# A convolutional attention block with a mixture of experts on one core: the last pair of batches taken batch by batch

## The chip, the core and the metric

One NeuronCore of a Trainium2 chip. The metric is the device time of one launch in microseconds, the median of several runs. Five engines work side by side, each on its own queue of instructions in order: TensorE (PE, matmuls into PSUM), VectorE (DVE), ScalarE (ACT), GpSimd (POOL, which reads and writes SBUF only) and SyncE (SP, which issues transfers). They meet by semaphores: an instruction adds to one when it is done, and a queue waits until one has reached a number.

## The reference, cut to what matters

Eight batches of 64 channels by 1024 tokens. First a channel attention, then a routed feed-forward part. In short, with the layer norms written out:

```python
x = x + conv_attention(layernorm_over_channels(x))      # per batch, 8 heads
t = to_tokens(x)                                        # (8, 1024, 64)
u = layernorm(t)
weights = softmax(mean(u, tokens) @ Wr + br)            # one routing row per batch
# scaled by capacity, softmax again, top 2 of 8 experts, softmax over the two
y = sum over the 2 experts of w_k * (gelu(u @ W1[k] + b1[k]) @ W2[k] + b2[k])
t = t + layernorm(y + u) * gamma + beta
```

The routing is by batch, so each batch uses two experts for all its tokens. In the last layer norm each token needs its mean of squares over the 64 channels (the mean itself is taken out by centred weights), and one reciprocal root of it.

## The kernel before, in words

Batches go in pairs, NP = 4 pairs p of batches b = 0, 1. In the feed-forward part a tile has 128 partitions: 64 channels of the first 512 tokens and 64 of the last 512; the 1024 columns are 512 of batch 0 and 512 of batch 1. A "step" is one expert k of one pair, step = 2p + k, eight in all. `up(step, b)` (L1155) multiplies by W1 into `h_ps[b]`, `gelu` (L387) brings it to `H` on ScalarE, `down(step, b)` (L1183) multiplies by W2 and adds into `y_ps`, on top of `residual3(p)` (L1169), which puts the residual there. The semaphore mm2 rises once a step, after the down of b = 1. GpSimd gathers the chosen experts' weights in advance (L470, L483).

When both experts of a pair are in `y_ps`, the last layer norm follows as a relay over engines:

- VectorE writes (y + c2) * gamma to `ZS` (`evac_z`, L828; L834), ScalarE squares y + c2 (`square_z`, L396; L406), the halves in opposite order.
- TensorE sums the squares over the channels (`rows3`, L1198; L996), ScalarE copies the rows (`evac_rows3`, L409; L413), TensorE turns them to columns with tokens on partitions (`columns3`, L1207; L1002).
- VectorE makes the variance (L840) and its reciprocal root by seven small instructions on 16 columns (`rsqrt`, L554: L557 to L567). GpSimd, and VectorE for the last pair, splits it in three bf16 parts (`split3`, L217: L220 to L223), TensorE turns these back (`turn3`, L1211; L1006), VectorE copies them (L853), and TensorE spreads them over the channels (`spread3`, L1048; L1011).
- VectorE scales `ZS` by the spread root (`scale_z`, L855; L858), and `add_residual` (L225; L230) adds T, which holds t + beta: GpSimd for pairs 0 to 2, VectorE for pair 3. Each addition releases the transfers of its batch (L263 on SyncE's queue; for the second half of the last pair's rows L436 on ScalarE's).

The order of TensorE's work is written by hand (L1232 to L1258): the relay of one pair is put between ups and downs of the next. After the last down there is no such work, and `keep_awake_at_end` (L1194) issues 7 and then 9 matmuls whose result nobody reads. The first layer norm of the feed-forward part is spread in another way: `spread2` (L1015; L1030) multiplies a root column, repeated 64 times as the weights, with the identity in float32.

## Time and profile before

| | us |
|---|---|
| median of 3 runs | 108.69 (108.67 to 108.73) |
| the profiled execution | 108.59 |
| its span (first to last instruction) | 106.8 |
| PE busy | 88.7 (83%) |
| DVE busy | 70.9 (66%) |
| ACT busy | 48.2 (45%) |
| POOL busy | 32.2 (30%) |

A busy share is an average over the span; what a late stage costs is read from its own rows. Times in the rows are from the span's start. In a timeline, rows of one kind that follow each other are merged with their count (x4), and the releaser in brackets is who ended the idle time before. PE rows overlap a little, since matmuls are pipelined; a float32 matmul has two records. The chain of waits gives each stretch of time to one instruction only.

### The profile page before, as it was taken

The numbers are of one execution on the slowest core, as the hardware profiler recorded it, in microseconds if no ns is written. First come the engines' busy times: TensorE is split into PE (matmuls) and PEld (weight loads), VectorE is DVE, ScalarE is ACT, GpSimd is POOL, SyncE is SP. The second block draws the span as 40 slices with busy tenths as digits, with TensorE's granted clock in tenths as the row PEclk, the third lists the DMA queues.
The fourth block names the chain that finished last, engine by engine and source line by source line (L and its number), as shares of the span: only waits on it lengthen the run. The fifth ranks groups of instructions, "written<-read, shape, count | busy, mean of one in ns | idle before, by whom it ended". The sixth has DMA issues, their size and how long they took to land.

```text
span 106.8 us, 2258 instructions
## 1 busy us (share of the span) xinstructions
PE 88.7 (83%) x748; PEld 47.8 (45%) x749; DVE 70.9 (66%) x258; ACT 48.2 (45%) x83; POOL 32.2 (30%) x77
## 2 busy tenths in 40 slices
PE   5967898998999999777976999599999999986200
PEld 1424776997665437355922237133333333242100
DVE  0098999842789978989999943714537256668920
ACT  0000946647321111103747899996795895510000
POOL 5000000005200000004428199956261900861400
PEclk9999999999999999999999999999999999999975
DMA  3899999400000000001420125680000080056065
GB/s 56 302 396 312 269 303 345 84 0 0 0 6 0 0 0 0 3 6 47 101 52 6 32 69 130 153 201 7 6 0 0 0 185 18 0 132 147 15 147 147
DMA packets 6554, 9.82 MB, mean 92 GB/s; under 512 B 1040, under 2 KB 3344, under 8 KB 6544
## 3 DMA queue, kind: packets, MB, share of 16 engines
q1 hardware_dynamic: 4848, 6.77, 24.1%
q10 hardware_dynamic: 1696, 2.92, 9.6%
q8 instruction: 6, 0.10, 0.4%
q14 instruction: 4, 0.03, 0.1%
HBM read 5.49 MB, written 2.10 MB: 71 GB/s over the span
## 4 chain that ended last, share of the span: by engine, by line
PE 58%; DVE 15%; ACTq 9%; ACT 7%; issue 5%; DVEq 1%
PE pC L1188 14%; PE pC L955 5%; ACTq L281 5%; PE pA L906 4%; PE pB L896 3%; PE pA L967 3%; PE pA L1163 3%; ACTq L276 3%; PE pB L1163 3%; PE pM L996 2%; DVE bst L644 2%; ACT SQ L406 2%; PE pC L1180 2%; PE pS L1030 2%; ACT U L290 2%
## 5 line engine op out<-in xcount | busy, mean ns | idle before, releaser
L457 POOL TENSOR_TENSOR LO<-UF,HI 128x512 f16<-128x512 f32 x8 | 9.2, 1157 | 23.5 <-ACT HI L324 22.6
L1188 PE MATMUL pC<-H,w2g 128*64 128x512 f32 x64 | 15.8, 602 | 0.0
L576 DVE BATCH_NORM_STATS2 bst<-XT 128x6 f32<-128x128 f32 x32 | 7.1, 282 | 5.2 <-DMA XT<-x_tok_dram 5.2
L230 POOL TENSOR_TENSOR XT<-XT,T 128x512 f32<-128x512 f32 x6 | 7.5, 1269 | 4.0 <-DVE XT L858 4.0
L1076 PE MATMUL pM<-wz 128*128 128x512 bf16 x25 | 7.1, 444 | 1.3 <-POOL wz L450 1.3
L393 ACT ACTIVATE H<-pA,b1s 128x1024 f32<-128x1024 f32 x6 | 6.7, 1111 | 2.5 <-PE pA L1163 2.3
L473 POOL COPY w1g<-w1hl 128x256 f16 x14 | 5.1, 403 | 8.1 <-issue 6.0
L324 ACT CAST HI<-UF 128x512 f16<-128x512 f32 x8 | 4.8, 619 | 6.0 <-DVE UF L677 6.0
L463 POOL TENSOR_TENSOR w1hl<-SQ,w1hl 128x512 f16<-128x512 f32 x2 | 2.3, 1154 | 17.2 <-DVE A L623 17.2
L644 DVE BATCH_NORM_STATS2 bst<-pA 128x6 f32<-128x128 f32 x32 | 6.9, 284 | 0.6 <-PE pA L967 0.5
L834 DVE TENSOR_SCALAR U<-pC,c,wsm 128x512 f32<-128x512 f32 x8 | 6.2, 801 | 1.4 <-PE pC L1188 0.9
L406 ACT ACTIVATE SQ<-pC,c 128x512 f32<-128x512 f32 x8 | 5.4, 685 | 3.8 <-PE pC L1188 3.0
L858 DVE TENSOR_TENSOR XT<-U,pS 128x512 f32<-128x512 f32 x6 | 4.1, 684 | 4.3 <-PE pS L1011 4.3
L638 DVE SCALAR_TENSOR_TENSOR T<-pC,cbs,X 128x512 f32<-128x512 f32 x8 | 5.7, 747 | 1.8 <-PE pC L955 1.8
L393 ACT ACTIVATE H<-pB,b1s 128x1024 f32<-128x1024 f32 x6 | 6.7, 1122 | 0.0
L1188 PEld LDWEIGHTS pC<-H,w2g 128*64 128x64 f32 x64 | 4.1, 136 | 5.9 <-issue 4.3
L331 ACT ACT_TABLE_LOAD x1 | 1.3, 1283 | 10.9 <-issue 10.9
L955 PE MATMUL pC<-U,MTs 64*64 64x512 f32 x32 | 6.1, 613 | 0.0
L290 ACT COPY U<-pA 128x1024 f32<-128x1024 f32 x4 | 4.0, 1012 | 3.4 <-PE pA L906 3.4
L319 ACT COPY SR<-pM 128x256 f32<-128x256 f32 x4 | 1.5, 372 | 9.0 <-PE pM L980 9.0
L967 PE MATMUL pA<-cst,T 128*128 128x128 f32 x32 | 5.0, 284 | 0.2 <-DVE bst L644 0.2
L594 DVE TENSOR_TENSOR UT<-XT,rt 128x512 f32<-128x512 f32 x8 | 5.1, 688 | 0.1
(219 smaller groups left out, 186.7 us busy)
## 6 DMA issues: line engine op xcount, KB each, us to landing
out_dram<-XT SPq DMA_DIRECT2D x14, 128.0 KB, 2.4
XT<-x_tok_dram SPq DMA_DIRECT2D x2, 512.0 KB, 9.3
X<-x_cha_dram SPq DMA_DIRECT2D x8, 128.0 KB, 11.0
X<-x_cha_dram ACTq DMA_DIRECT2D x8, 128.0 KB, 10.9
ST<-HI SPq DMA_DIRECT2D x6, 128.0 KB, 2.4
ST<-LO SPq DMA_DIRECT2D x6, 128.0 KB, 2.4
XT<-x_tok_dram SPq DMA_DIRECT2D x2, 256.0 KB, 4.8
XT<-x_tok_dram ACTq DMA_DIRECT2D x2, 256.0 KB, 5.1
```

Of the source, the lines that this page charges most:

```text
L230: engine.tensor_tensor(OUT[:, p, cols], V[:, p, cols], T[:, p, cols], ALU.add).then_inc(s_fin[2 * p + h], 1)
L393: nc.scalar.activation(H[:, step % 2, b, :], h_ps[b][:, :], ACT.Gelu, bias=bias, scale=1.0 / (S_U * S_W)).then_inc(s["gelu"], 1)
L406: nc.scalar.activation(SQ[:, p % 2, cols], y_ps[:, cols], ACT.Square, bias=c2[:, 2 * p + b:2 * p + b + 1]).then_inc(s["sq3"], 1)
L457: nc.gpsimd.tensor_tensor(LO[:, p, cols], UF[:, p, cols], HI[:, p, cols], ALU.subtract).then_inc(s["lo"], 1)
L576: return nc.vector.bn_stats(bst[:, p, j, :], XT[:, p, j * P:(j + 1) * P].rearrange("p (b c) -> p c b", b=2))
L644: last = nc.vector.bn_stats(bst2[:, p, j, :], tt[:, j * P:(j + 1) * P].rearrange("p (h c) -> p c h", h=2))
L834: nc.vector.tensor_scalar(ZS[:, p, cols], y_ps[:, cols], c2[:, i:i + 1], w("gamma"), ALU.add, ALU.mult).then_inc(s["zs"], 1)
L955: last = mm(half(cv[:, b * HALF:(b + 1) * HALF], h), half(MTs[:, p, :], b), half(U[:, p, h * HALF:(h + 1) * HALF], b), start=True, stop=True)
L967: last = nc.tensor.transpose(tt[:, j * P:(j + 1) * P], T[:, p, j * P:(j + 1) * P], cf("ident"))
L1076: mm(pM[:, :], wz[:, 0:P], wz[:, :], start=True, stop=True)
L1163: last = mm(h_ps[b][:, h * HALF:(h + 1) * HALF], w1g[h * C:(h + 1) * C, p % 2, k, b, a, :], src[h * C:(h + 1) * C, p, b * HALF:(b + 1) * H ...
L1188: last = mm(half(y_ps[:, b * HALF:(b + 1) * HALF], h), w2g[:, p % 2, b, k, :], H[:, step % 2, b, h * HALF:(h + 1) * HALF], start=False, st ...
```

## The change

Pair 3 is taken by batches. `unit(step, i)` gives for steps 6 and 7 the batch by the step and the expert by i: step 6 is both experts of batch 6 (the pair's first), step 7 both of batch 7. So batch 6 is whole in `y_ps` after step 6's downs. The relay of pair 3 is then run once per batch, in pieces of 128 columns (`rows_last`, `columns_last`, `variance_last`), its moments in `ps_last`. The reciprocal root is one GpSimd instruction per batch, a power with exponent -0.5 (`root_last`), and TensorE spreads it in the way of `spread2` (`spread_last`), without the split, the turn and the copy. `keep_awake_at_end` is gone. In step 7 `columns3` comes before down(6,0); after the last up the order of TensorE is written out. ScalarE takes over the evacuation of batch 7's `ZS` (`evac_z_last`), which needs gamma * c2 as its bias: one new VectorE instruction makes it (gc2) before the first `evac_z`. The additions: both of pair 2 go from GpSimd to VectorE, the first of pair 3 (batch 6) goes from VectorE to GpSimd.

```diff
@@ -143,6 +143,8 @@
         gtab = sb("gtab", [P, 1])
+        mhalf = sb("mhalf", [P, 1])
+        gc2 = sb("gc2", [P, 1])
@@ -163,6 +165,11 @@
             return ap.rearrange("p (q h b) -> p h q b", h=2, b=2)
+        def unit(step, i):
+            p, n = step // TOP, step % TOP
+            return (p, n, i) if p < NP - 1 else (p, i, n)
@@ -192,8 +199,9 @@
-        ps_rt3 = [q[0:3 * G2, 0:P // 2].bitcast(BF16) for q in (pS, pS, pS, pB)]
-        rb3 = [[pS[:, :], pS[:, :]]] * (NP - 1) + [[pB[:, HALF:N], pA[:, HALF:N]]]
+        ps_rt3 = [pS[0:3 * G2, 0:P // 2].bitcast(BF16)] * (NP - 1)
+        rb3 = [[pS[:, :], pS[:, :]]] * (NP - 2) + [[pS[:, :], pB[:, HALF:N]], [pA[:, 0:HALF], pA[:, HALF:N]]]
+        ps_last = [pM[:, 0:P], pB[:, 0:P]]
         ps_lg = [pM, pA[:, 0:HALF]]
@@ -207,7 +215,7 @@
         names = ("ones wz iota onesm brzz brz wrz wrd w1f wcp wcv bvz bvd gram gs tb u p1 p1s s_ps sms exs a_sb b1 b1s mt mts "
-                 "cbs conv t st sr w1p w1h w1l w2p w2v pow1 tt bt sc red2 pow2 rb hi lo lgm lg lr rexp1 rexp2 "
+                 "cbs conv t mh gc st sr w1p w1h w1l w2p w2v pow1 tt bt sc red2 pow2 rb hi lo lgm lg lr rexp1 rexp2 "
                  "half_tanh rx1 rx2 rx3 wkd top w1g "
@@ -378,19 +386,34 @@
+            def square_last(b):
+                act.wait_ge(s["mm2"], TOP * NP - 1 + b)
+                cols = slice(b * HALF, (b + 1) * HALF)
+                nc.scalar.activation(SQ[:, 1, cols], y_ps[:, cols], ACT.Square,
+                                     bias=c2[:, B - 2 + b:B - 1 + b]).then_inc(s["sq3"], 1)
+            def evac_rows_last(b):
+                act.wait_ge(s["row3"], NP + b)
+                act.wait_ge(s["mom3"], NP - 2)
+                nc.scalar.copy(RW[:, 1, b * P:(b + 1) * P], ps_last[b]).then_inc(s["rw3"], 1)
+            def evac_z_last():
+                act.wait_ge(s["gc"], 1)
+                nc.scalar.activation(ZS[:, NP - 1, HALF:N], y_ps[:, HALF:N], ACT.Identity, bias=gc2[:, :],
+                                     scale=w("gamma")).then_inc(s["zs"], 1)
             def gelu_bias(p, k, b):
                     return w("b1T")[:, bass.ds(first_expert(k, b), 1)]
-                act.wait_ge(s["b1d"], k + 1)
+                act.wait_ge(s["b1d"], TOP)
                 return b1s[:, k, 2 * p + b:2 * p + b + 1]
-            def gelu(p, k, b):
-                step = TOP * p + k
-                bias = gelu_bias(p, k, b)
-                act.wait_ge(s["mm1"], 2 * step + b + 1)
+            def gelu(step, i):
+                bias = gelu_bias(*unit(step, i))
+                act.wait_ge(s["mm1"], 2 * step + i + 1)
                 if step >= 2:
                     act.wait_ge(s["mm2"], step - 1)
-                nc.scalar.activation(H[:, step % 2, b, :], h_ps[b][:, :], ACT.Gelu, bias=bias,
+                nc.scalar.activation(H[:, step % 2, i, :], h_ps[i][:, :], ACT.Gelu, bias=bias,
                                      scale=1.0 / (S_U * S_W)).then_inc(s["gelu"], 1)
@@ -416,12 +439,12 @@
                     square_z(p - 1)
-                gelu(p, k, 0)
+                gelu(step, 0)
                 if k == 1 and p >= 1:
                     half_tanh()
-                gelu(p, k, 1)
+                gelu(step, 1)
                 if step == 0:
@@ -429,8 +452,10 @@
                     add_beta(p)
-            square_z(NP - 1)
-            evac_rows3(NP - 1)
+            for b in range(2):
+                square_last(b)
+                evac_rows_last(b)
+            evac_z_last()
             for b in range(2):
@@ -490,7 +515,16 @@
+            def root_last(b):
+                pool.wait_ge(s["mh"], 1)
+                pool.wait_ge(s["red3"], NP + b)
+                cols = slice(b * G2 // 2, (b + 1) * G2 // 2)
+                nc.gpsimd.tensor_tensor(r3[:, NP - 1, cols], v3[:, NP - 1, cols],
+                                        mhalf[:, 0:1].broadcast_to([P, G2 // 2]), ALU.pow).then_inc(s["pow3"], 1)
             nc.gpsimd.memset(wrbd[:, :], 0.0).then_inc(s["wrz"], 1)
+            nc.gpsimd.memset(mhalf[:, :], -0.5).then_inc(s["mh"], 1)
             nc.gpsimd.memset(brz[:, :], 0.0).then_inc(s["brzz"], 1)
@@ -535,8 +569,9 @@
                     add_residual(nc.gpsimd, pool, p - 1, 1)
-            add_residual(nc.gpsimd, pool, NP - 2, 0)
-            add_residual(nc.gpsimd, pool, NP - 2, 1)
+            root_last(0)
+            root_last(1)
+            add_residual(nc.gpsimd, pool, NP - 1, 0)
@@ -824,6 +859,7 @@
             dve.wait_ge(s["c2d"], 1)
+            nc.vector.tensor_tensor(gc2[:, :], c2[:, B - 1:B], w("gamma"), ALU.mult).then_inc(s["gc"], 1)
@@ -857,25 +893,34 @@
-            for p in range(NP):
-                if p < NP - 1:
-                    evac_z(p)
+            def evac_z_first():
+                dve.wait_ge(s["sq3"], 2 * NP - 1)
+                nc.vector.tensor_scalar(ZS[:, NP - 1, 0:HALF], y_ps[:, 0:HALF], c2[:, B - 2:B - 1], w("gamma"),
+                                        ALU.add, ALU.mult).then_inc(s["zs"], 1)
+            def variance_last(b):
+                dve.wait_ge(s["mom3"], NP + b)
+                nc.vector.tensor_scalar(v3[:, NP - 1, b * G2 // 2:(b + 1) * G2 // 2].rearrange("p (q r) -> p q r", r=2),
+                                        ps_last[b].rearrange("p (q r) -> p q r", r=32)[:, :, 0:2], 1.0, EPS_T,
+                                        ALU.mult, ALU.add).then_inc(s["red3"], 1)
+            for p in range(NP - 1):
+                evac_z(p)
                 if p >= 1:
                     scale_z(p - 1, 0)
-                if 1 <= p < NP - 1:
                     scale_z(p - 1, 1)
                 rstd3(p)
-                if p == NP - 2:
-                    evac_z(NP - 1)
-                if p == NP - 1:
-                    dve.wait_ge(s["pow3"], NP)
-                    dve.wait_ge(s["rt3"], NP - 2)
-                    split3(nc.vector, link, p % 2, 1, r3[:, p:p + 1, :], s["s3"])
                 rows3(p)
+            evac_z_first()
+            variance_last(0)
+            scale_z(NP - 2, 0)
             scale_z(NP - 2, 1)
+            variance_last(1)
+            add_residual(nc.vector, dve, NP - 2, 0)
+            add_residual(nc.vector, dve, NP - 2, 1)
             scale_z(NP - 1, 0)
+            dve.wait_ge(s["zs"], 2 * NP)
             scale_z(NP - 1, 1)
-            add_residual(nc.vector, dve, NP - 1, 0)
             add_residual(nc.vector, dve, NP - 1, 1)
@@ -1047,8 +1092,8 @@
                 pe.wait_ge(s["rr3"], p + 1)
-                if 2 * p + h >= 1 and p < NP - 1:
-                    pe.wait_ge(s["vv"], 2 * p + h)
+                if 2 * p + h >= 1:
+                    pe.wait_ge(s["vv"], min(2 * p + h, 2 * NP - 4))
                 spread(rb3[p][h], h * CH // 2, CH // 2, p).then_inc(s["rb3"], 1)
@@ -1152,15 +1197,15 @@
-            def up(step, b):
-                p, k = step // TOP, step % TOP
-                pe.wait_ge(s["w1g"], 2 * step + b - 1)
-                pe.wait_ge(s["gelu"], 2 * (step - 1) + b + 1)
+            def up(step, i):
+                p, k, b = unit(step, i)
+                pe.wait_ge(s["w1g"], 2 * (TOP * p + k) + b - 1)
+                pe.wait_ge(s["gelu"], 2 * (step - 1) + i + 1)
                 for n, (a, src, done) in enumerate(((0, HI, s["hi"]), (1, HI, s["hi"]), (0, LO, s["lo"]))):
                     for h in range(2):
-                        last = mm(h_ps[b][:, h * HALF:(h + 1) * HALF],
+                        last = mm(h_ps[i][:, h * HALF:(h + 1) * HALF],
                                   w1g[h * C:(h + 1) * C, p % 2, k, b, a, :],
@@ -1180,20 +1225,16 @@
-            def down(step, b):
-                p, k = step // TOP, step % TOP
-                pe.wait_ge(s["gelu"], 2 * step + b + 1)
-                pe.wait_ge(s["g2"], 2 * step + b + 1)
+            def down(step, i):
+                p, k, b = unit(step, i)
+                pe.wait_ge(s["gelu"], 2 * step + i + 1)
+                pe.wait_ge(s["g2"], 2 * (TOP * p + k) + b + 1)
                 for h in range(2):
                     last = mm(half(y_ps[:, b * HALF:(b + 1) * HALF], h), w2g[:, p % 2, b, k, :],
-                              H[:, step % 2, b, h * HALF:(h + 1) * HALF],
+                              H[:, step % 2, i, h * HALF:(h + 1) * HALF],
                               start=False, stop=(k == TOP - 1))
-                if b == 1:
+                if i == 1:
                     last.then_inc(s["mm2"], 1)
-            def keep_awake_at_end(n):
-                for _ in range(n):
-                    mm(h_ps[0][:, 0:HALF], cb("identb"), cb("sel")[:, 0:HALF], start=True, stop=True)
@@ -1210,9 +1251,32 @@
                 pe.wait_ge(s["s3"], p + 1)
-                if 1 <= p < NP - 1:
+                if p >= 1:
                     pe.wait_ge(s["vv"], 2 * p)
                 turn(ps_rt3[p], p % 2).then_inc(s["rt3"], 1)
+            def rows_last(b):
+                pe.wait_ge(s["sq3"], 2 * NP - 1 + b)
+                if b == 0:
+                    pe.wait_ge(s["red3"], NP - 1)
+                for q in range(4):
+                    last = mm(ps_last[b][32 * q:32 * (q + 1), :], cf("mean2"),
+                              SQ[:, 1, b * HALF + q * P:b * HALF + (q + 1) * P], start=True, stop=True)
+                last.then_inc(s["row3"], 1)
+            def columns_last(b):
+                pe.wait_ge(s["rw3"], NP + b)
+                nc.tensor.transpose(ps_last[b], RW[:, 1, b * P:(b + 1) * P], cf("ident")).then_inc(s["mom3"], 1)
+            def spread_last(b):
+                pe.wait_ge(s["pow3"], NP + b)
+                for k in range(CH // 2):
+                    for h in range(2):
+                        i = b * G2 // 2 + 2 * k + h
+                        last = mm(half(rb3[NP - 1][b][:, k * P:(k + 1) * P], h),
+                                  r3[:, NP - 1, i:i + 1].broadcast_to([P, C]), cf("ident"), start=True, stop=True)
+                last.then_inc(s["rb3"], 1)
@@ -1229,33 +1293,36 @@
-            for step in range(3, TOP * NP + 4):
+            for step in range(3, TOP * NP):
                 q, odd = (step - 5) // TOP, step % TOP
-                if step < TOP * NP:
-                    for b in range(2):
-                        up(step, b)
-                if step > TOP * NP and odd and q + 1 < NP:
-                    rows3(q + 1)
+                for i in range(2):
+                    up(step, i)
                 if odd and q >= 0:
                     spread3(q, 0)
-                if step < TOP * NP and odd and q + 1 >= 0:
+                if odd:
                     rows3(q + 1)
-                if step <= TOP * NP:
-                    if step % TOP == 1:
-                        residual3(step // TOP)
-                    down(step - 1, 0)
-                if step > TOP * NP and odd and q + 1 < NP:
+                    residual3(step // TOP)
+                if step == TOP * NP - 1:
                     columns3(q + 1)
+                down(step - 1, 0)
                 if odd and q >= 0:
                     spread3(q, 1)
-                if step < TOP * NP and odd and q + 1 >= 0:
+                if odd and step < TOP * NP - 1:
                     columns3(q + 1)
-                if step <= TOP * NP:
-                    down(step - 1, 1)
-                if not odd and 0 <= (step - 4) // TOP < NP:
-                    if step >= TOP * NP:
-                        keep_awake_at_end(7 if step == TOP * NP else 9)
+                down(step - 1, 1)
+                if not odd and step >= 4:
                     turn3((step - 4) // TOP)
+            down(TOP * NP - 1, 0)
+            turn3(NP - 2)
+            rows_last(0)
+            down(TOP * NP - 1, 1)
+            columns_last(0)
+            spread3(NP - 2, 0)
+            spread3(NP - 2, 1)
+            rows_last(1)
+            columns_last(1)
+            spread_last(0)
+            spread_last(1)
```

## Rows read from the trace of the kernel before

**Rows 1.** The page: the chain that ended last, by engine

```profile
PE 58%; DVE 15%; ACTq 9%; ACT 7%; issue 5%; DVEq 1%
```

**Rows 2.** The chain in order of time: start us, us, what

```profile
65.59 0.90 PE pM L1030 x16
...
88.43 0.33 PE pS L1011 x4
...
89.13 2.73 PE pC L1188 x12
...
92.01 1.46 PE pA L1196 x6
...
95.39 1.26 DVE nwt L557
```

**Rows 3.** Timeline, 87 to 93 us: start, us, engine line op [idle before <-releaser]

```profile
87.23 0.37 ACT L413 COPY RW<-pM 128x256 f32<-128x256 f32 x1
...
88.80 0.69 DVE L858 TENSOR_TENSOR XT<-U,pS 128x512 f32<-128x512 f32 x1 [1.81 <-PE pS L1011]
...
89.40 0.17 DVE L840 TENSOR_SCALAR v<-pM 128x16 f32<-128x16 f32 x1
...
91.10 0.20 POOL L220 CAST R<-r 128x16 bf16<-128x16 f32 x1 [5.41 <-DVE r L567]
...
92.03 2.50 POOL L230 TENSOR_TENSOR XT<-XT,T 128x512 f32<-128x512 f32 x2
```

**Rows 4.** Timeline, the last scalings and additions

```profile
99.66 0.67 DVE L858 TENSOR_TENSOR XT<-U,pB 128x512 f32<-128x512 f32 x1
99.82 1.27 POOL L230 TENSOR_TENSOR XT<-XT,T 128x512 f32<-128x512 f32 x1 [3.22 <-DVE XT L858]
100.26 0.67 DVE L858 TENSOR_TENSOR XT<-U,pA 128x512 f32<-128x512 f32 x1
100.86 1.38 DVE L230 TENSOR_TENSOR XT<-XT,T 128x512 f32<-128x512 f32 x2
```

**Rows 5.** Timeline, pair 0's evacuation, squares and moments

```profile
67.12 0.81 DVE L834 TENSOR_SCALAR U<-pC,c,wsm 128x512 f32<-128x512 f32 x1
...
67.76 1.26 ACT L406 ACTIVATE SQ<-pC,c 128x512 f32<-128x512 f32 x2
...
69.07 0.64 PE L996 MATMUL pM<-SQ,cst 128*32 128x256 f32 x8 [1.21 <-ACT SQ L406]
```

**Rows 6.** Timeline of POOL alone, at 67 us and at 78 us

```profile
67.06 1.16 POOL L457 TENSOR_TENSOR LO<-UF,HI 128x512 f16<-128x512 f32 x1
...
78.07 1.04 POOL L489 TENSOR_TENSOR w2g<-w2c,wk 128x64 f32<-128x64 f32 x4
```

**Rows 7.** Timeline, 48.6 to 51 us

```profile
48.66 1.16 POOL L457 TENSOR_TENSOR LO<-UF,HI 128x512 f16<-128x512 f32 x1 [21.20 <-ACT HI L324]
...
49.01 0.89 DVE L746 TENSOR_TENSOR rout<-rout,rsm 128x64 f32<-128x64 f32 x1
...
50.90 0.22 DVE L752 TENSOR_TENSOR rout<-rout,rsm 128x64 f32<-128x64 f32 x1
```

**Rows 8.** Groups by form on POOL: busy us, mean ns | idle before

```profile
L221 POOL TENSOR_TENSOR rd<-r,R 128x16 f32<-128x16 f32 x3 | 0.7, 218 | 0.2
```

**Rows 9.** SyncE's last two transfers: duration ns, first and last start; landing

```profile
L263 SPq DMA_DIRECT2D out_dram<-XT x2: 852/933/1014, 102.3 to 103.2; - x2
...
DMA to landing us min/median/max: 3.2/3.2/3.3
```

**Rows 10.** ScalarE's two transfers: the same columns

```profile
L436 ACTq DMA_DIRECT2D out_dram<-XT x2: 522/542/562, 101.7 to 102.3; - x2
...
DMA to landing us min/median/max: 2.4/3.1/3.8
```

**Rows 11.** Busy us by stretch: PE PEld DVE ACT POOL, PEclk, DMA share, GB/s

```profile
68.00:70.00 2.00, 0.93 (x12) 0.41 (x14) 0.81 (x1) 2.00 (x4) 1.33 (x2) 1.00 0.74 175
...
100.00:104.00 4.00, 0.00 (x0) 0.00 (x0) 2.24 (x4) 0.00 (x0) 1.09 (x1) 0.88 0.40 91
```

## The prediction

> **What bounds the kernel now.** I read three views in this order: the chain of waits, to see who sets the end; the timeline of the last 20 us, to see each step of the tail; then the rows of transfers and of two earlier stretches. The page's chain gives TensorE over half of the span [rows 1], but the last 15 us are another thing. Down to 91.86 us the chain is TensorE, matmul after matmul: three half downs of 0.91 us each end it [rows 2]. From there to the last addition, which ends at 102.24, it is a relay: keep-awake matmuls, moments, the root on VectorE, its split and turn, spread, scaling, addition. The whole root and turn of pair 3 stands between 95.39 and the first scaling by it at 99.66, 4.27 us [rows 2, 4]. In it one instruction on 16 columns takes 1.26 us [rows 2]; it stood beside a GpSimd addition of pair 2 and got through when that ended. The last transfer is issued at 103.2, 0.9 us after the last addition, because SyncE was still issuing pair 2's, whose second half GpSimd added only from 99.82 to 101.09 [rows 4, 9]. It lands 3.2 us later, 0.4 us before the span's end.
>
> The profiled execution took 108.59 us against a median of 108.69; its span is 106.8, so 1.79 us lie around it. All times below are on the span's clock of before; the sum ends at 108.59 and I forecast with the same 1.79.
>
> **Before the last pair.** Steps up to 6 keep their order and sizes on all engines (two experts of one batch cost what one expert of two batches does: same shapes, and the last gathers, pair 3's, are done at 79.1 [rows 6], two us before their first use). The memset of the -0.5 column lies where GpSimd waits for the first loads: nothing. One edit here is not free. gc2 is a new VectorE instruction between the last normalising multiply and pair 0's evacuation, which starts at 67.12 [rows 5]. By size it would cost 0.05 to 0.2 us. But both its inputs are in SBUF, and GpSimd is in a subtraction that reads SBUF from 67.06 to 68.22 [rows 6]. What that does is seen at 49.01: a VectorE tensor_tensor of 64 columns with both inputs in SBUF took 0.89 us, ending 0.08 after the GpSimd subtraction that had begun before it; the same form with GpSimd idle took 0.22 [rows 7]. So gc2 ends at about 68.25 and the evacuation starts about 1.1 us late. ScalarE's square of that half, which waits for it, starts at 69.05 instead of 68.34 (0.4 us of the delay was waiting for ScalarE anyway: its two squares run 67.76 to 69.02), and TensorE's moments, which had idled 1.21 us for that square [rows 5], start 0.7 us late. From there the chain is TensorE and the same evacuations, with no slack before 86 us. I take **+0.7 us**; the other end is 0.05.
>
> The Trainium skill, page "SBUF — State Buffer", section "Who interferes with whom", states this as a rule: a VectorE instruction with two SBUF inputs contends with a GpSimd instruction that reads SBUF, and the later one blocks for the whole of the other. The trace's 0.89 against 0.22 us agrees. Without the rule gc2 would be priced at 0.05, and the forecast would be 0.65 us lower.
>
> **The tail, step by step** (without the 0.7). Step 7 issues the turned moments of pair 2 before down(6,0) rather than after. They wait for the row copy that ends at 87.60 [rows 3], take 0.37 (the gap between the rows at 88.76 and 89.13 [rows 2]) and let down(6,0) start at 88.0; it ends near 88.95, and the spread of pair 1's second half (0.33) at 89.28 instead of 88.76. VectorE's multiply of that half waits for it, and the root of pair 2 stands behind that multiply, so its moments being early buys nothing: multiply at 89.3, moments at 89.9, and the split on GpSimd, done by 92.05 before (the addition behind it starts at 92.03 [rows 3]), at 92.6. TensorE meanwhile does down(6,1) and down(7,0), to 91.1, and now has turn3(2) next. It **waits 1.5 us** there, with down(7,1) queued behind it. Then turn 0.25, rows_last(0) 0.4 (half the columns of the 0.64 us row [rows 5]; bounds 0.3 to 0.64), down(7,1) to 94.15, columns_last(0) to 94.4, both spreads of pair 2 to 95.05. Before, the last down ended at 91.86; this costs 2.3 us, and the rest has to earn it back.
>
> Batch 7: square 0.69 to 94.9, rows_last(1) 95.05 to 95.45, copy of 128 columns 0.26 (bound 0.37 [rows 3]) and transposes to 96.1, variance on VectorE to 96.3. VectorE has by then scaled both halves of pair 2 (94.75 to 96.0; 512-column instructions follow each other every 0.60 us, 99.66 to 100.26 [rows 4]). The square, rows and copy of batch 6 lie under down(7,1).
>
> GpSimd splits pair 2 to 92.6, adds pair 1's residual for 2.50 [rows 3] to 95.05, and only then takes root_last(0), though its variance is there at 94.6. The **price X of a power** on 8 columns is in no row. The nearest rows: a plain GpSimd subtraction of 16 columns takes 0.22 [rows 8], and the whole root of a pair on VectorE takes 1.70 (89.40 to the cast at 91.10 [rows 3]). I take 0.6: eight values a partition are few, so the fixed part of 0.2 weighs most, with some 50 ns for each value; both ends stay for the range. root_last(1) is ready at 96.35, but VectorE has just started the first addition of pair 2 (two SBUF inputs), to 96.9. Either one goes first; in both orders the two follow each other: power to 96.9 + X, second addition to 97.5 + X, scaling of batch 6 to 98.1 + X. TensorE's spread_last(1) needs 0.9 (16 matmul records in the same form [rows 2]) and ends at 97.9 + X, in time for scaling of batch 7. GpSimd's addition of batch 6 runs from 98.15 + X for 1.27 [rows 4]; VectorE's own addition of batch 7, ready at 98.7 + X, again has two SBUF inputs and ends 0.6 after it, at **100.0 + X**. If VectorE isn't held there, GpSimd's is last, at 99.4 + X.
>
> With X = 0.6 and the 0.7 of gc2 the last addition ends at 101.3, against 102.24. What goes: the stalled instruction of 1.26 us and, behind it, the ten small instructions, turn, copy and spread up to the scaling (96.65 to 99.66, 3.0 us [rows 2, 4]); what comes: the 1.5 us wait of TensorE, two additions on VectorE ahead of the last scalings, gc2.
>
> **After the last addition.** Before it is 4.56 us to the span's end. Pair 2's four transfers now start at 97.7 and 98.8, and are issued when the last pair's come, so SyncE no longer runs 0.9 us late. ScalarE's second transfer is the other end: it was issued at 102.3, in time, and took 3.8 [rows 10]. Bounds 3.6 to 4.4; I take 3.9, since four transfers share the end and not six. Span 101.3 + 3.9 = 105.2, time **107.0 us**, 1.6 us or 1.5% faster.
>
> **Rivals.**
> (1) gc2 isn't held, since it has a single column or gets its read in first: 106.35. For it: no row is so small. Against: rows 7, and that GpSimd's subtraction begins 0.06 us before it. Chance 0.25; with X near 0.22 and no hold at the last addition, this reaches 105.4.
> (2) The power is dear, and the kernel slower. Above X = 1.2 the two powers follow each other without a gap other than an addition, and the end is 98.8 + 2X; before is met at 102.2, X = 1.7. Both powers stand in line on GpSimd behind 2.5 us of additions, and VectorE's additions with two SBUF inputs are held beside them, so nothing hides them. At X = 2.5 the time is 103.8 + 0.7 + 3.9 + 1.8 = 110.2. For it: a power is a function and not one pass of an adder; no row shows it. Against: only 8 values a partition. Chance 0.17.
> (3) TensorE falls to 1.2 GHz in the thinner tail, as the fillers are gone: from 92.6 on turn, rows, down, columns and spreads double, 2.9 us on the path, 109.9. Against it: the granted clock is full in 68 to 70 us at 0.93 of 2 us busy, and falls only well after the last matmul of before (0.88 over 100 to 104) [rows 11]. Chance 0.08.
> (4) The batches don't do what they should: batch 6's early start is eaten by the wait at turn3(2). That is in the sum already. If the sum is short of another 1.6 us of such waits the result is no change: chance 0.05.
> The forecast, X between 0.2 and 1.7 with gc2 held, has 0.45.
>
> **How the numbers follow.** A measurement of this kernel tells some 0.2% (0.2 us) from no change. Faster: 0.45 + 0.25 and the part of (2) just below the break-even and of (3), 0.03: 0.73. Same 0.07. Slower: most of (2) and (3), 0.20. The range goes from 105.5 (rival 1 with small X) to 109.2 (X = 2.0), which leaves out most of (3) and the upper half of (2), and a little below.
>
> **What the profile after would show.** gc2's row at about 1.1 us, and moments of pair 0 at 69.8; if it is 0.2 and they stand at 69.1, rival 1. TensorE idle some 1.5 us before pair 2's turn. Two powers on GpSimd: their duration is X itself, the first right behind pair 1's additions. VectorE's last addition recorded at 1.2 to 1.3 us beside GpSimd's. The last transfer issued within 0.2 us of the last addition. A granted clock below 1 between 90 and 98 would be rival 3. The prediction is wrong if the power costs over 1.7 us, or if the chain before 86 us moves by anything but gc2.

## The result

Over 4 runs the changed kernel took 107.06 us (median), the kernel before 108.71 on the same chip; the ratio is 0.9843 (in brackets here and below, its 95% interval: [0.9825, 0.986]), 1.6% faster. The forecast was 107.0. That the number came out is in good part luck: a power cost 1.65 us and more where the forecast had 0.6, and what follows the powers was shorter than forecast by nearly as much as that adds.

The profiled execution of the changed kernel took 109.52 us, with a mean granted clock of 0.954 and TensorE at 1.2 GHz in two stretches; the others on that chip had 0.992 to 0.995 and spans of 105.2 to 105.3. So the tail is read from other executions, and this one for what happens at 67 to 76 us. Its page, the chain by engine and the clock in 40 slices (compare [rows 1]: GpSimd is new in the chain):

```profile
PE 55%; DVE 14%; ACTq 9%; ACT 8%; POOL 6%; issue 5%; POOLq 0%; DVEq 0%
...
PEclk9999999999999999999999999957999999999755
```

Its timeline at pair 0's evacuation, which answers [rows 5] and [rows 6]. L862 is the new multiply, gc2; L429 the squares, L1041 the moments:

```profile
67.20 1.11 DVE L862 TENSOR_TENSOR gc<-c,wsm 128x1 f32<-128x1 f32 x1
...
69.06 0.69 ACT L429 ACTIVATE SQ<-pC,c 128x512 f32<-128x512 f32 x1 [0.54 <-DVE U L870]
...
69.80 0.64 PE L1041 MATMUL pM<-SQ,cst 128*32 128x256 f32 x8 [1.86 <-ACT SQ L429]
```

One column takes 1.11 us, the moments start at 69.80 instead of 69.07, and TensorE's wait for them grew from 1.21 to 1.86 us. Busy us by stretch of the same execution (the columns of [rows 11]):

```profile
68.00:70.00 2.00, 0.20 (x4) 0.16 (x8) 1.75 (x3) 1.46 (x3) 1.40 (x2) 1.00 0.71 167
70.00:72.00 2.00, 2.00 (x14) 0.62 (x8) 0.00 (x0) 2.00 (x4) 1.26 (x4) 0.62 0.86 200
72.00:74.00 2.00, 2.00 (x8) 0.59 (x6) 0.22 (x2) 1.07 (x2) 1.17 (x5) 0.53 0.11 26
74.00:76.00 2.00, 2.00 (x16) 0.50 (x12) 1.18 (x7) 0.34 (x1) 0.47 (x3) 1.00 0.00 0
```

The column behind POOL's is the granted clock. TensorE is busy for 0.20 of 2 us (before 0.93 [rows 11]), and then works for some three microseconds at half clock. That is some 1.6 us of the execution's extra 2.4 (its tail starts that much later than in the next run's trace); the rest is the last spread, 1.82 us instead of 1.09. The thin stretch alone does not settle it: in the next run TensorE is busy for 0.18 of the same 2 us, and the clock stays at 1.00.

### The profile page after: what moved, and what is told of

The parts are those of the page before. It is cut to its first block, busy times and chain, and to the rows that moved or that the text cites. A ratio compares the mean times of both kernels' runs of the same rounds, so it can differ in the third digit from the quotient of the medians.

```text
span 107.7 us, 2282 instructions
## 1 busy us (share of the span) xinstructions
PE 89.9 (84%) x764; PEld 48.8 (45%) x764; DVE 68.6 (64%) x248; ACT 49.2 (46%) x85; POOL 34.4 (32%) x79
## 4 chain that ended last, share of the span: by engine, by line
PE 55%; DVE 14%; ACTq 9%; ACT 8%; POOL 6%; issue 5%; POOLq 0%; DVEq 0%
PE pC L1233 12%; PE pC L1000 5%; ACTq L289 5%; PE pA L951 4%; PE pB L941 3%; PE pA L1012 3%; POOL r L523 3%; PE pA L1208 3%; ACTq L284 3%; PE pB L1208 3%; DVE bst L679 2%; POOL XT L238 2%; DVE U L870 2%; PE pS L1075 2%; PE pC L1225 2%
## 5 line engine op out<-in xcount | busy, mean ns | idle before, releaser
L1233 PE MATMUL pC<-H,w2g 128*64 128x512 f32 x64 | 17.0, 637 | 0.0
L1121 PE MATMUL pM<-wz 128*128 128x512 bf16 x25 | 7.8, 482 | 1.3 <-POOL wz L475 1.3
L238 POOL TENSOR_TENSOR XT<-XT,T 128x512 f32<-128x512 f32 x5 | 6.3, 1269 | 0.1
L894 DVE TENSOR_TENSOR XT<-U,pS 128x512 f32<-128x512 f32 x5 | 3.4, 687 | 4.4 <-PE pS L1056 4.4
L1121 PEld LDWEIGHTS pM<-wz 128*128 128x128 bf16 x25 | 2.8, 119 | 5.4 <-issue 2.8
L429 ACT ACTIVATE SQ<-pC,c 128x512 f32<-128x512 f32 x6 | 4.1, 686 | 1.9 <-DVE U L870 1.2
```

Of the source, the lines that this page charges most:

```text
L238: engine.tensor_tensor(OUT[:, p, cols], V[:, p, cols], T[:, p, cols], ALU.add).then_inc(s_fin[2 * p + h], 1)
L1121: mm(pM[:, :], wz[:, 0:P], wz[:, :], start=True, stop=True)
L1233: last = mm(half(y_ps[:, b * HALF:(b + 1) * HALF], h), w2g[:, p % 2, b, k, :], H[:, step % 2, i, h * HALF:(h + 1) * HALF], start=False, st ...
```

## Experiments

### The same kernel again

> The changed kernel once more, for a clean record of its tail: 107.1 us, span 105.3, granted clock full to the last matmul. If the power is the size of what the first record shows (two in 3.48 us), the two powers take 1.5 to 1.9 us each here too, and the last addition ends near 101.8. If those 3.48 us were mostly a wait for the port (VectorE's additions with two SBUF inputs), one of the two, the one with no such addition beside it, is under 1 us.

Measured: 107.96 us (107.79 to 108.12) against 108.49 of before on that chip, ratio 0.9951 [0.9935, 0.9968]. The tail of its profiled execution (107.79 us, span 106.0); it answers [rows 3] and [rows 4]. L1047 turns the moments of pair 2, L894 scales, L238 adds, L523 is the power, L903 the variance of a batch, L1277 the last spreads:

```profile
88.39 0.44 PE L1047 MATMUL pM<-cst,RW 128*128 128x128 f32 x2
...
90.20 0.69 DVE L894 TENSOR_TENSOR XT<-U,pS 128x512 f32<-128x512 f32 x1 [2.48 <-PE pS L1056]
...
93.43 2.50 POOL L238 TENSOR_TENSOR XT<-XT,T 128x512 f32<-128x512 f32 x2
...
93.53 0.24 PE L1051 MATMUL pS<-cstb,R 128*48 128x128 bf16 x1 [1.49 <-POOL R L231]
...
95.42 0.17 DVE L903 TENSOR_SCALAR v<-pM 128x8 f32<-128x8 f32 x1 [0.69 <-PE pM L1269]
...
95.89 3.47 POOL L523 TENSOR_TENSOR r<-v,mhalf 128x8 f32<-128x8 f32 x2
...
97.09 0.17 DVE L903 TENSOR_SCALAR v<-pB 128x8 f32<-128x8 f32 x1
...
97.17 1.29 DVE L238 TENSOR_TENSOR XT<-XT,T 128x512 f32<-128x512 f32 x2
...
99.42 1.66 PE L1277 MATMUL pA<-cst,r 128*64 128x128 f32 x16 [0.73 <-POOL r L523]
...
99.50 1.27 POOL L238 TENSOR_TENSOR XT<-XT,T 128x512 f32<-128x512 f32 x1
...
101.18 0.69 DVE L894 TENSOR_TENSOR XT<-U,pA 128x512 f32<-128x512 f32 x1 [1.76 <-PE pA L1277]
101.91 0.69 DVE L238 TENSOR_TENSOR XT<-XT,T 128x512 f32<-128x512 f32 x1
```

TensorE waits 1.49 us for pair 2's split, as forecast. The chain then is GpSimd's: two additions, then two powers of 1.64 and 1.85 us (minimum and maximum of L523), though batch 6's variance was there 0.3 us earlier and batch 7's some 0.25 us before the second power. The first power has no VectorE addition beside it until its last 0.35 us and still takes 1.64: the price is its own. The last spread takes 1.66 us, where 1.09 is the size at full clock.

### gc2 elsewhere, and gc2 alone

```diff
-            nc.vector.tensor_tensor(gc2[:, :], c2[:, B - 1:B], w("gamma"), ALU.mult).then_inc(s["gc"], 1)
...
                 rstd3(p)
+                if p == 1:
+                    nc.vector.tensor_tensor(gc2[:, :], c2[:, B - 1:B], w("gamma"), ALU.mult).then_inc(s["gc"], 1)
                 rows3(p)
```

> The changed kernel with the one-column multiply moved from before pair 0's evacuation to behind pair 1's root, where GpSimd does not read a long tile. Theory (0.7 us is lost to its wait for GpSimd's subtraction, and nothing after it gives it back): 0.7 us faster than the changed kernel, 106.4; pair 0's moments start at 69.1. Rival (the delay is made up for by slack before the tail): no difference, 107.1. In its new place the multiply takes 0.1 to 0.2 us.

> The kernel before with only the one-column multiply added where the change has it; nobody reads its result. Theory: 0.7 us slower than before, 109.4, its row 1.1 us long. Rival (slack): 108.7.

Measured: with the late gc2 106.49 us, 1.47 below the run above on the same chip (0.9813 [0.9796, 0.9829] against before). The kernel before with gc2 added: 109.22 against 108.49, 1.0109 [1.0036, 1.0182]. First two rows from the timeline with the late gc2, then the same view of the kernel before with gc2:

```profile
68.98 0.64 PE L1042 MATMUL pM<-SQ,cst 128*32 128x256 f32 x8 [1.20 <-ACT SQ L429]
...
82.05 0.15 DVE L913 TENSOR_TENSOR gc<-c,wsm 128x1 f32<-128x1 f32 x1
```

```profile
66.97 1.11 DVE L828 TENSOR_TENSOR gc<-c,wsm 128x1 f32<-128x1 f32 x1
...
69.57 0.64 PE L998 MATMUL pM<-SQ,cst 128*32 128x256 f32 x8 [1.86 <-ACT SQ L407]
```

The same instruction takes 0.15 us at 82 and 1.11 at 67. Alone in the kernel before it costs 0.73 us: nothing behind it makes up for the delay. The 1.47 us of the first comparison are more than that. Of the 1.40 us between the two traces' last additions, 0.18 are there at 65 us already, ahead of gc2 (the same normalising multiply starts at 65.73 and 65.55), 0.65 come in with gc2, and 0.57 with the last spread, which took 1.09 us in the late version, at full clock, against 1.66. The next run looks at that spread.

### Filling TensorE's waits

```diff
             down(TOP * NP - 1, 0)
+            keep_awake(pA[:, 0:HALF], 6)
             turn3(NP - 2)
...
             spread_last(0)
+            keep_awake(pM[:, :], 3)
             spread_last(1)
```

> The changed kernel with matmuls nobody reads in TensorE's two waits of the tail: six before pair 2's turn, three between the two last spreads. Theory (the 107.9 us of the repeated run are the 107.1 of the first plus the last spread at 1.2 GHz, 1.66 us instead of 0.87): granted clock full to the last matmul, the last spread 0.9 us, 107.1 us. Rival (the clock has nothing to do with it, the 0.8 us belong to something else): the time stays at 107.9.

Measured: 107.13 us, 0.9864 [0.9844, 0.9883], on a chip where the changed kernel with idle-time powers added (below) took 107.84. First the last spread of that kernel with idle-time powers, where the granted clock is 0.50 from 100 to 102 us. Then the timeline of this execution, span 105.3; then SyncE's transfers and their landing, then ScalarE's (this answers [rows 9] and [rows 10]):

```profile
99.12 1.97 PE L1285 MATMUL pA<-cst,r 128*64 128x128 f32 x16 [0.75 <-POOL r L524]
```

```profile
99.29 1.09 PE L1281 MATMUL pA<-cst,r 128*64 128x128 f32 x16
...
99.36 1.27 POOL L238 TENSOR_TENSOR XT<-XT,T 128x512 f32<-128x512 f32 x1
...
100.50 0.69 DVE L894 TENSOR_TENSOR XT<-U,pA 128x512 f32<-128x512 f32 x1 [1.21 <-PE pA L1281]
...
101.22 0.69 DVE L238 TENSOR_TENSOR XT<-XT,T 128x512 f32<-128x512 f32 x1
```

```profile
L271 SPq DMA_DIRECT2D out_dram<-XT x6: 466/533/602, 97.8 to 101.9; - x6
...
DMA to landing us min/median/max: 2.2/2.4/2.5
```

```profile
L461 ACTq DMA_DIRECT2D out_dram<-XT x2: 503/518/534, 100.7 to 101.9; - x2
...
DMA to landing us min/median/max: 2.9/2.9/2.9
```

So the spread at half clock, 1.97 us instead of 1.09, accounts for the 0.7 us between these two. That the fillers made the difference isn't shown: there is one execution without them on this chip, and the version with the late gc2 has the same waits in its tail (1.49, 0.54 and 0.73 us), no fillers, and ended its last spread at full clock, with all four of its runs within 0.15 us. One of the four filled runs took 108.70 us. This execution has the span of the four shorter runs of the first chip, and I take it as the clean record of the changed kernel's tail: last addition ends at 101.91, both last transfers start at 101.9, the span ends 3.4 us after the addition.

### The power replaced by a multiply, and powers of several sizes

The first leaves the root out: `ALU.pow` becomes `ALU.mult` in `root_last`. The second adds these to the changed kernel, into a scratch tile, where GpSimd is idle:

```diff
+            for n, op in ((8, ALU.pow), (8, ALU.pow), (1, ALU.pow), (16, ALU.pow), (32, ALU.pow), (32, ALU.mult)):
+                nc.gpsimd.tensor_tensor(scr[:, at:at + n], ones_m[:, at:at + n],
+                                        mhalf[:, 0:1].broadcast_to([P, n]), op)
+                at += n
```

> The changed kernel with the power replaced by a multiply of the same shape; so the last pair's root is left out (its result is a product, not a root). Theory (both powers are on the path behind GpSimd's additions): the multiply takes 0.2 us, and the kernel gains nearly twice the price of a power until VectorE's chain binds: at 1.5 us each, 1.3 to 2.0 us, 105.1 to 105.8. Rival (the powers lie under VectorE's two additions, and the path is VectorE's): under 0.5 us, 106.6 or more.

> The changed kernel with six extra GpSimd instructions into a scratch tile, in its idle stretch before 48 us: powers of 8, 8, 1, 16 and 32 columns and a multiply of 32. If the price is mostly a fixed part (a call), 1 column takes over 1 us and 32 columns under 2.5. If it is by value, 1 column takes about 0.35 us, 8 take 1.65, 16 about 3.1 and 32 about 6. If the first use pays for loading code, the first of the two powers of 8 is longer than the second by a microsecond or more. The multiply takes 0.25 us. The time stays as it is, as GpSimd has 20 us of idle time there.

Measured: 106.45 us with multiplies (0.9803 [0.9787, 0.9819]); against the changed kernel on that chip 1.5 us less, but that includes the clock's part. Against the changed kernel with its last spread at full clock (107.06 on the first chip, 107.13 with fillers) the multiplies save 0.6 to 0.7. The profiled execution (107.77 us) had the stretch behind gc2 at half clock, as the first one of the changed kernel; its tail is at full clock. Timeline of that tail:

```profile
97.21 0.20 POOL L523 TENSOR_TENSOR r<-v,mhalf 128x8 f32<-128x8 f32 x1
...
98.49 1.30 DVE L238 TENSOR_TENSOR XT<-XT,T 128x512 f32<-128x512 f32 x2
98.72 0.52 POOL L523 TENSOR_TENSOR r<-v,mhalf 128x8 f32<-128x8 f32 x1 [1.31 <-DVE v L903]
...
100.47 1.27 POOL L238 TENSOR_TENSOR XT<-XT,T 128x512 f32<-128x512 f32 x1 [1.23 <-DVE XT L894]
101.23 1.05 DVE L238 TENSOR_TENSOR XT<-XT,T 128x512 f32<-128x512 f32 x1
```

A multiply in the power's place takes 0.20 us, and 0.52 when it meets VectorE's additions. The gain of taking 2.8 us of power away is far from 2.8: batch 7's variance and VectorE's two additions bind now, and VectorE's last addition, which meets GpSimd's, takes 1.05 instead of 0.69. The last transfers of both batches now start within 0.5 us of each other and land in 2.9 to 3.2 us, so the span ends 3.7 us after the last addition, not 3.4. So what the prediction had in its tail is there (VectorE's additions ahead of the last scalings, the hold at the last addition, four transfers at the end), but it decides at 0.2 us a root and not at 1.65. The expectation's 105.1 to 105.8 was missed by that.

Sizes, from the timeline and from the groups by form on GpSimd:

```profile
27.23 1.69 POOL L544 TENSOR_TENSOR scr<-ones_m,mhalf 128x8 f32<-128x8 f32 x1
...
33.91 5.41 POOL L544 TENSOR_TENSOR scr<-ones_m,mhalf 128x32 f32<-128x32 f32 x1
```

```profile
L544 POOL TENSOR_TENSOR scr<-ones_m,mhalf 128x8 f32<-128x8 f32 x2 | 3.3, 1664 | 0.0
L544 POOL TENSOR_TENSOR scr<-ones_m,mhalf 128x16 f32<-128x16 f32 x1 | 2.9, 2900 | 0.0
L544 POOL TENSOR_TENSOR scr<-ones_m,mhalf 128x1 f32<-128x1 f32 x1 | 0.6, 562 | 0.0
```

From 1 to 32 columns: (5.41 - 0.56) / 31 = 0.156 us for each value and 0.40 fixed. The first use costs 0.05 more (1.69 against 1.64), so the extra microsecond that the expectation allowed for loading code does not appear.

### Pair 2's root first; its moments where they were

```diff
                 if p >= 1:
                     scale_z(p - 1, 0)
+                if 1 <= p < NP - 2:
                     scale_z(p - 1, 1)
                 rstd3(p)
+                if p == NP - 2:
+                    scale_z(p - 1, 1)
```

That is on top of the late gc2. The other run, also with the late gc2, puts `columns3` of step 7 back behind down(6,0).

> The kernel with the late gc2, and on VectorE pair 2's root before the scaling of pair 1's second half instead of behind it. Its moments have been there since 88.0, so the root ends near 89.7 instead of 91.6. Theory (the path is root, split, GpSimd's additions, the two powers): TensorE's wait before pair 2's turn is gone, GpSimd's additions end 1.9 us earlier, the first power starts 1.8 us earlier, at 93.2, and the time falls from 106.5 by 1.7 to 2.1 us, to 104.4 to 104.8. Rival (VectorE's tail is the bound, and the wait of TensorE was free): under 0.5 us, 106.0 or more.

> The kernel with the late gc2, and pair 2's moments turned where they were before the change, behind down(6,0). Theory (turning them early only delays the spread of pair 1's second half, and with it the root behind it): root and split 0.5 us earlier, 106.0 us. Rival (the first power waits for its variance as much as for GpSimd): the gain stops at 0.2 to 0.3 us, since the variance of batch 6 is ready 0.3 us before the power starts; 106.2.

Measured: root first 104.75 us, 0.965 [0.9634, 0.9666], which is 1.7 below the late gc2. Moments back 106.21 us (105.75 to 106.76), 0.9771 [0.9723, 0.982]: two runs at 105.8 and two at 106.7, and in the profiled one of the latter the last spread takes 1.81 us. In the trace the first power starts at 94.56 instead of 95.06 with the late gc2 alone, though this execution was 0.16 us later at 86 us: the theory's 0.5 us, and not the rival's 0.2 to 0.3. The two lower runs are 0.7 below the late gc2, on another chip; with two levels of clock in four runs I leave the size in the time open. Root first, timeline (L875 pair 2's variance, L1055 its turn):

```profile
88.03 0.17 DVE L875 TENSOR_SCALAR v<-pM 128x16 f32<-128x16 f32 x1 [1.14 <-PE pM L1051]
...
90.65 2.50 POOL L238 TENSOR_TENSOR XT<-XT,T 128x512 f32<-128x512 f32 x2
...
91.03 0.22 PE L1055 MATMUL pS<-cstb,R 128*48 128x128 bf16 x1
...
93.22 3.63 POOL L523 TENSOR_TENSOR r<-v,mhalf 128x8 f32<-128x8 f32 x2
...
98.83 0.69 DVE L238 TENSOR_TENSOR XT<-XT,T 128x512 f32<-128x512 f32 x1
```

The variance at 88.03 instead of 89.98 carries through to the first power (93.22 instead of 95.06) and to the last addition (98.83 instead of 100.51). So the early moments of the change pay only if VectorE takes them early, and this version beats both kernels: 3.5% under before.

### One root on each engine

On top of that: batch 7's root by the seven instructions on VectorE, and the first addition of pair 2 on GpSimd.

```diff
             variance_last(1)
-            add_residual(nc.vector, dve, NP - 2, 0)
-            add_residual(nc.vector, dve, NP - 2, 1)
+            rsqrt(v3[:, NP - 1, G2 // 2:G2], G2 // 2, r3[:, NP - 1, G2 // 2:G2], s["powv"])
             scale_z(NP - 1, 0)
+            add_residual(nc.vector, dve, NP - 2, 1)
```

> The kernel with the root of pair 2 first, and batch 7's root by the seven instructions on VectorE (about 1.4 us) instead of the power on GpSimd; GpSimd takes the first addition of pair 2 in its place. The two roots then run side by side instead of one behind the other. Theory (at 1.65 us a power, the second one is what the last spread waits for): root of batch 7 done at 96.2 instead of 96.85, VectorE fuller by the seven instructions and emptier by one addition; last addition at 98.7 instead of 99.5, 104.0 us against 104.75. Rival (VectorE is full by now, so what leaves GpSimd comes back there): 104.6 to 105.0.

Measured: 105.81 us, 0.9747 [0.9728, 0.9765], 1.1 slower than root first (on another chip; 0.965 against before there); outside both expectations.

```profile
94.99 1.26 POOL L238 TENSOR_TENSOR XT<-XT,T 128x512 f32<-128x512 f32 x1
...
95.13 1.15 DVE L594 TENSOR_TENSOR nwt<-nwt 128x8 f32<-128x8 f32 x1
96.31 0.17 DVE L595 TENSOR_TENSOR nwt<-nwt,v 128x8 f32<-128x8 f32 x1
...
97.96 1.65 POOL L238 TENSOR_TENSOR XT<-XT,T 128x512 f32<-128x512 f32 x1 [1.70 <-DVE XT L893]
...
99.27 0.89 DVE L238 TENSOR_TENSOR XT<-XT,T 128x512 f32<-128x512 f32 x1
```

The root's second instruction (two SBUF inputs, eight columns) meets GpSimd's addition and takes 1.15 us. I had moved an addition next to a root, the very thing that cost 1.26 us in the kernel before. The last addition ends at 100.16 instead of 99.52, which is 0.6 of the 1.1 us. The rest lies behind it: GpSimd's last addition ends only 0.55 us before VectorE's, both batches' transfers share the end, and the span ends 3.8 us after the last addition instead of 3.4.

### Waits in the kernel before

```diff
+            pool.wait_ge(s["pow3"], NP)
             add_residual(nc.gpsimd, pool, NP - 2, 0)
```

The second run waits on `s["s3"]` instead, for the split.

> The kernel before, with one wait more: GpSimd starts pair 2's first addition only when the last root is done. It takes away what the root's first instruction stood beside (1.25 us instead of 0.18). Theory: 1.0 us faster than before, 107.5, if the two additions, now later, cost nothing; 0.3 us less if VectorE's first addition of pair 3 has to wait for GpSimd's second of pair 2, which is still beside it. Rival (that instruction was long for another reason): its row stays at 1.2 us and the time at 108.5 or above.

> As the run with the wait on the last root, but GpSimd waits until VectorE has split it too (four more small instructions, two of them with both inputs in SBUF). Theory (VectorE is held wherever such an instruction meets a GpSimd addition; the first wait only moved the meeting from the root's first instruction to the split's second): no small instruction over 0.25 us in the last root and split, spread 1.0 us earlier; the later additions of pair 2 give 0.2 to 0.3 of it back beside VectorE's last ones: 107.7 to 107.9. Rival (the time lies elsewhere and the additions of pair 2 give all of it back): 108.4 again.

Measured: 108.42 us, 0.9984 [0.9975, 0.9994], and 107.68 us, 0.9915 [0.9899, 0.9932]. Timeline of the first (L221 is the split's second instruction), then of the second:

```profile
95.28 0.17 DVE L558 TENSOR_SCALAR nwt<-v 128x16 uint32<-128x16 uint32 x1
...
96.79 1.26 POOL L230 TENSOR_TENSOR XT<-XT,T 128x512 f32<-128x512 f32 x1 [2.37 <-DVE r L568]
96.95 1.13 DVE L221 TENSOR_TENSOR rd<-r,R 128x16 f32<-128x16 f32 x1
```

```profile
97.10 0.18 DVE L221 TENSOR_TENSOR rd<-r,R 128x16 f32<-128x16 f32 x1
...
97.65 2.58 POOL L230 TENSOR_TENSOR XT<-XT,T 128x512 f32<-128x512 f32 x2 [3.09 <-DVE R L223]
```

The first wait frees the root (0.17 us for the instruction that took 1.25) and hands the same meeting to the split. The second removes it: 0.87 us for one line, over half of what the whole change gave. The root's first instruction is a tensor_scalar with one tensor input, in SBUF, and it was held as long as the two-input ones, so the hold is not a matter of two inputs only.

## Why the prediction came out

**gc2, +0.7: right.** It took 1.11 us for the instruction, moments at 69.80, and 0.73 us alone in the kernel before. The step that had no row of its own (would a single column be held too?) is answered: it is. Rival 1 falls.

**TensorE's wait of 1.5 us before pair 2's turn: right in size** (1.49), and the times around it too: with the 0.7 added, the forecast had batch 6's variance done at 95.3 and the first power starting at 95.75; the filled run has 95.46 and 95.76.

**The price of a power: wrong, and this is the step that failed.** I took 0.6 us, near the row of a plain subtraction [rows 8], with "some 50 ns for each value"; it is 156 ns a value and 0.40 fixed, 1.65 for eight. The upper bound, taken from a whole root on VectorE [rows 3], was the near one, and the second power, beside VectorE's additions, lies above it at 1.85. I chose by the count of values, where I should have asked what each one costs. The two took 3.5 us together, 1.74 each, so the prediction's own sign of being wrong (over 1.7 us) was met, and yet the kernel was not slower, for the next two reasons.

**What was not where I put it.** At 1.65 us the prediction's own formula, 98.8 + 2X, gives 102.1 and with gc2 102.8 for the last addition, and 108.5 us for the kernel, no change; it ended at 101.9. The right price in the forecast's own sum would have spoiled its result, so the 107.0 is luck: 1.5 us more for the powers, against 0.9 less in what stands around them and 0.5 less after the last addition. The formula kept an addition of VectorE's between the two powers, and GpSimd's last addition as a hold on VectorE's. Neither happened: the powers ran back to back from 95.76 to 99.23 over VectorE's two additions (1.29 us for both, not held), and GpSimd's last addition, from 99.36 to 100.63, was over before VectorE's began at 101.22. The longer powers left the two additions apart. The multiply run, with short roots, shows the hold (1.05 us for the last addition). So the break-even of 1.7 us a power was too low as well: two powers of 3.47 us in all left the kernel 1.5 us ahead.

**After the last addition: too dear by 0.5.** I took 3.9 us, from landings of 3.2 and 3.8 [rows 9, 10]; it is 3.4, with 2.4 and 2.9. The mechanism was right (pair 2's transfers are out of the way, SyncE issues at 101.9 with no delay), but even four transfers is too many: GpSimd's early addition of batch 6 lets its two go 1.2 us ahead, so only two share the end. Where four did, in the multiply run and the one with a root on each engine, it was 3.7 and 3.8 us, near the 3.9 that I took; the size was right for a case that did not arise. Of the span's 1.5 us gain, 1.2 come from here (4.56 to 3.39 us) and 0.3 from the last addition (102.24 to 101.91). The forecast had 0.7 and 0.9: late additions and early landings cancelled to 0.1 us.

**The clock: a rival that is true in part.** Not everything from 92.6 on was at half clock; in the repeated run the granted clock is 1.00 up to 98 us and 0.50 from 100 to 102. What it touched in some executions is the last spread, 1.66 to 1.97 us instead of 1.09, and in some the stretch behind gc2. The spread cost 0.6 to 0.9 us on two of three chips that ran this tail (on one of them in a single execution), and nothing on the first except in the profiled execution. The row I held against it, full clock with 0.93 of 2 us busy [rows 11], became 0.20 of 2 us through gc2, a link that I had not made. The times speak for it: of 23 executions with gc2 in its early place (in five kernels, one of them the kernel before with gc2 alone) four were 1.3 to 2.5 us above their kernel's median, and of 68 without it none was more than 0.6 above. The two of the four that were profiled, of the changed kernel and of the multiply run, have the clock at 0.5 to 0.6 from 70 to 74 us. So the early gc2 seems to have a second price, paid now and then. Why the clock falls in one execution and not in the next is not settled by these runs.

## What to carry to other kernels

Before putting an elementwise instruction that reads and writes only SBUF on VectorE (with two inputs, or with one, as the root's first), or one that reads SBUF on GpSimd, look in the timeline at what the other engine does at that moment: a single column can cost a microsecond, and a wait that parts the two can be worth more than a new algorithm, if it covers all of the small instructions and not just the first. An operation that no row shows should be measured in an idle stretch at several sizes before a path is built on it. When a step is made to finish early, check that its consumer isn't queued behind something late: here one reordering on VectorE was worth as much as the rest of the change.

## What the runs showed of the hardware that I had not expected

- A GpSimd power costs 0.40 us and 0.156 for each value of a partition, against 0.23 us in all for a multiply of 8 to 32 values (0.20 in the multiply run).
- The hold between VectorE and GpSimd goes both ways. GpSimd's multiply of 8 columns took 0.52 us instead of 0.20 when it met VectorE's addition already running (98.72 after 98.49), its addition 1.65 instead of 1.27 (97.96 after 97.80). The Trainium skill, page "SBUF — State Buffer", section "Who interferes with whom", says that issue order decides who blocks; these rows agree. But running powers did not hold VectorE: two additions with two SBUF inputs each took 1.29 us together beside them, which is one alone (0.69) and the 0.60 between the starts of such instructions [rows 4]. It was the second power that grew, to 1.85 and, in the run with pair 2's root first, 1.96 us.
- TensorE's granted clock dropped to 1.2 GHz after thin stretches (0.20 of 2 us busy, or the tail's waits of 0.5 to 0.7 us between spreads), in some executions of a kernel and not in others. Whether nine filler matmuls keep it up in the tail is open: three of four filled runs ended at 107.1 us, but so did four of five unfilled ones on the first chip.
